# A decoder layer on one core: the opening's first attention row is served in another order

## The reference

```python
def _L0_attn_ref(x, Wv, bv, Wo, bo):
    p = jnp.einsum('bsd,ed->bse', x, Wv) + bv
    p = p.reshape(b, s, h, dk).transpose(0, 2, 1, 3)       # h = 16, dk = 8
    q = k = v = p
    attn = jax.nn.softmax(jnp.einsum('bhqd,bhkd->bhqk', q, k) / math.sqrt(dk), axis=-1)
    out = jnp.einsum('bhqk,bhkd->bhqd', attn, v)
    out = out.reshape(b, s, h * dk)                        # heads are not moved back: rows mix heads
    return jnp.einsum('bsd,ed->bse', out, Wo) + bo
x = x + _L0_attn_ref(_layernorm(x), Wv, bv, Wo, bo)
x = x + _L0_xattn_ref(_layernorm(x), ctx, ctx)             # 16 heads, no projections
x = x + _L0_ffn_ref(_layernorm(x), ...)                    # shared expert and the best of 7, SwiGLU
```

## Time and profile before

| | us |
|---|---|
| median of 3 runs (all) | 404.37 (403.18, 404.37, 407.61) |
| the profiled execution | 406.06 |
| its span, first to last instruction | 403.8 |
| TensorE busy in the span | 392.3 (97%) |
| VectorE, ScalarE, GpSimd busy | 309.7, 297.1, 283.1 |

### The profile page before, as it was taken

How to read it: one execution, slowest core, us unless ns; L and a number is a source line. 1 busy time by engine, 2 the same in 40 slices (tenths; PEclk the granted TensorE clock), 3 DMA queues, 4 the chain that set the end, 5 groups by cost and what they waited for, 6 DMA issues and landing times.

```text
span 403.8 us, 16282 instructions
## 1 busy us (share of the span) xinstructions
PE 392.3 (97%) x5549; PEld 309.9 (77%) x5550; DVE 309.7 (77%) x847; ACT 297.1 (74%) x685; POOL 283.1 (70%) x476
## 2 busy tenths in 40 slices
PE   8989999999999999899999999999999999999996
PEld 5556666666666666566666666999999999999996
DVE  7759999999999999899999987775444454455444
ACT  7568999999999999799999967622224666766651
POOL 7756888888888888688888744367777464444442
PEclk9999999999999999999999999999999999999999
DMA  6254656776777677675645400012223454520001
GB/s 105 48 81 61 100 94 99 134 117 123 126 132 123 118 122 135 124 124 98 79 54 61 36 22 5 0 48 87 87 86 101 106 144 142 143 89 21 30 32 55
DMA packets 176325, 35.22 MB, mean 87 GB/s; under 512 B 145587, under 2 KB 174646, under 8 KB 176256
## 3 DMA queue, kind: packets, MB, share of 16 engines
q1 hardware_dynamic: 71296, 21.43, 24.7%
q10 hardware_dynamic: 102144, 6.81, 16.2%
q0 software_dynamic: 2816, 6.10, 4.3%
HBM read 20.86 MB, written 15.67 MB: 90 GB/s over the span
## 4 chain that ended last, share of the span: by engine, by line
PE 80%; DMA 8%; DVE 5%; ACT 2%; issue 2%; SPq 1%; ACTq 0%; POOL 0%; DVEq 0%; POOLq 0%
PE psum L928 20%; PE psum L681 13%; PE psum L690 13%; PE psum L1033 10%; PE psum L702 8%; DMA attention_out<-on_s 3%; DMA orow<-attention_out 3%; PE psum L712 3%; PE psum L780 2%; PE psum L669 2%; PE psum L812 1%; PE psum L785 1%; PE psum L819 1%; PE psum L1085 1%; SPq L198 1%
## 5 line engine op out<-in xcount | busy, mean ns | idle before, releaser
L1743 DVE TENSOR_TENSOR gT<-gT,psum 128x384 f32<-128x384 f32 x66 | 36.6, 554 | 63.9 <-ACT gT L1375 38.1
L472 POOL TENSOR_TENSOR k_s<-pT,hmask_sb 128x1024 f32<-128x1024 f32 x32 | 60.9, 1902 | 17.2 <-issue 14.5
L642 POOL DMA_INDIRECT out<-yrow,token x38 | 37.0, 973 | 39.1 <-DVE yrow L1877 34.2
L1375 ACT ACTIVATE gT<-psum 128x384 f32<-128x384 f32 x66 | 32.1, 487 | 39.3 <-PE psum L928 38.6
L1033 PE MATMUL psum<-wdn_sb,gT 128*128 (+1 forms) x414 | 57.5, 275 | 0.0
L928 PE MATMUL psum<-fhT,wtile 128*128 128x128 f32 x456 | 57.1, 275 | 0.0
L928 PEld LDWEIGHTS psum<-fhT,wtile 128*128 128x128 f32 x456 | 53.9, 192 | 0.0
L1033 PEld LDWEIGHTS psum<-wdn_sb,gT 128*128 128x128 f32 x414 | 51.7, 192 | 0.2 <-DVE gT L1743 0.2
L928 PE MATMUL psum<-hT_all,wup_sb 128*128 128x128 f32 x384 | 48.2, 276 | 0.0
L1484 DVE TENSOR_REDUCE mx_s<-psum 128x16 f32<-128x1024 f32 x33 | 40.4, 1225 | 9.0 <-PE psum L681 6.3
L690 PEld LDWEIGHTS psum<-id_sb,pr_x 128*128 128x128 f32 x248 | 27.3, 141 | 24.5 <-ACT pr_x L1135 24.1
(11 more groups left out here) (199 smaller groups left out, 872.2 us busy)
## 6 DMA issues: line engine op xcount, KB each, us to landing
sorted_rows<-nowhere_row SPq DMA_DIRECT2D x38, 130.0 KB, 3.6
ring<-sorted_rows SPq DMA_DIRECT2D x30, 130.0 KB
wup_sb<-in_wup SPq DMA_DIRECT2D x14, 176.0 KB, 2.6
orow<-attention_out SPq DMA_DIRECT2D x31, 64.0 KB
ring<-in_ctxv ACTq DMA_DIRECT2D x60, 32.0 KB, 4.1
cross_keys<-in_ctxk ACTq DMA_DIRECT2D x14, 128.0 KB, 3.2
ring<-cross_keys SPq DMA_DIRECT2D x112, 16.0 KB
rows_all<-in_x ACTq DMA_DIRECT2D x10, 128.0 KB, 3.2
```

The source lines that it names most:

```text
L472: nc.gpsimd.tensor_tensor(k_s[:], pT[:].rearrange("p (b k) -> p b k", b=NB).unsqueeze(2).broadcast_to([P, NB, HG, S]), hmask_sb[:, 0:HG].u ...
L642: pool.indirect_dma_start(out=out, out_offset=bass.IndirectOffsetOnAxis(ap=token[p][:, 0:1], axis=0), in_=yrow[p][:, :], in_offset=None, b ...
L1743: nc.vector.tensor_tensor(g, g, ps_up[k][:, 0:CH * P], ALU.mult).then_inc(sem("f_g"), 1)
```

## The change

Four things, all in steps 3 and 4 of the opening, with line numbers moving by a few:

- SyncE stores both halves of units 0 and 1; ScalarE's `second_store` in the opening goes.
- VectorE writes `on_s` of unit 1 ahead of both subtractions of step 4, and puts `attention_added(0)` between them.
- TensorE does `project(0)` ahead of unit 2's transposes and `query(0)` right behind `new_row`; ScalarE does `output(0)` ahead of unit 2's exponentials and `query(0)` right behind `turned`.
- The fillers at the end of step 3 and those ahead of `query(0)` in step 4, two calls of two products each, go.

```diff
--- before.py
+++ after.py
@@ SyncE, body
                 if live("out") and u["out"] < U - 1:
                     sp.wait_ge(sem("s_on"), at(u["out"]))
                     store_half(sp, u["out"], 0)
+                    if t < STEADY:
+                        store_half(sp, u["out"], 1)
@@ TensorE, opening
+                if live("q"):
+                    project(u["q"])
                 if live("soft_s"):
                     turn("s", u["soft_s"], 0)
                     turn("s", u["soft_s"], 1)
-                if live("q"):
-                    project(u["q"])
                 if live("xT"):
                     new_row(u["xT"])
+                if live("q"):
+                    query(u["q"])
                 if live("soft_s"):
                     self_weighed(u["soft_s"])
...
                 if live("soft_s"):
                     turn_back("s", u["soft_s"])
-                if t == LAG["q"]:
-                    keep_clock(2, bank[3])
-                if live("q"):
-                    query(u["q"])
...
-                    keep_clock((1, 4, 4, 2)[t], bank[3])
+                    keep_clock((1, 4, 4, 0)[t], bank[3])
@@ ScalarE, opening
+                if live("q"):
+                    output(u["q"])
                 if live("soft_s"):
                     exp("s", u["soft_s"], 0)
                     exp("s", u["soft_s"], 1)
-                if live("out"):
-                    second_store(u["out"])
-                if live("q"):
-                    output(u["q"])
-                if live("soft_s"):
                     turned("s", u["soft_s"], 0)
                     turned("s", u["soft_s"], 1)
+                if live("q"):
+                    query(u["q"])
                 bulk_of_step(t)
...
                 if live("out"):
                     cross_values(u["out"], 1)
-                if live("q"):
-                    query(u["q"])
@@ VectorE, opening
                 if live("out"):
                     invert("s", u["out"])
-                if live("out") and t < LAG["q"]:
                     normalise("s", u["out"])
                 if live("soft_s"):
                     soften("s", u["soft_s"], 0)
-                    soften("s", u["soft_s"], 1)
-                if live("out") and t >= LAG["q"]:
-                    normalise("s", u["out"])
                 if live("q"):
                     attention_added(u["q"])
+                if live("soft_s"):
+                    soften("s", u["soft_s"], 1)
+                if live("q"):
                     query_moments(u["q"])
```

## The result

The changed kernel takes 408.76 us (median of 20 runs, 405.46 to 412.56) where the kernel before, beside it, takes 405.21 us (20 runs, 403.18 to 408.42): a ratio of 1.0075, 95% interval [1.0049, 1.0101]. It is slower by some 3 us, three quarters of a per cent (3.5 us between the two medians), and the time lies outside the predicted range (403.2 to 407.4). The three runs of before on which the prediction stood (404.37) lay 0.84 us under the median of twenty.

A forecast was written before the change was run, and what follows sets the result against it. The prediction took TensorE's pace in the loop to bound the kernel, with the opening's chain through unit 0's row ahead of it. +2.32 (dependency) − 0.99 (sooner row) = +1.33 us on 404.37 gave 405.7 us, range 403.2 to 407.4.

The forecast's parts named there:

- dependency: Step 4: unit 2's softmax now stands behind unit 0's projection, so unit 3's self scores end later after the row, +2.32 us.
- sooner row: Unit 0's attention output, stored by SyncE alone, is read back and turned at 25.55 instead of 26.54, -0.99 us.
- T: Start of `turn_output(0)`, when TensorE turns unit 0's row: 26.54 before, predicted 25.55, between 25.1 and 26.05.
- the fillers' 0.86 us: TensorE time of the fillers on the chain behind unit 0's row; predicted to buy nothing, as it lies beside unit 3's softmax.
- unit 1's sooner row: Unit 1, normalised ahead of step 4's subtractions, lands near 31.7 rather than 32.84; predicted to buy nothing.
- the softmax of unit 3 ends last alone: Step 5: of three chains that ended together, only unit 3's softmax still ends last; its second transposes start at 34.85, not 33.52.
- the two ahead of T fill an idle wait and cost nothing: Fillers at the end of step 3, while TensorE waits for unit 0's row: no gain counted for leaving them out.
- the rival of the clock: TensorE's clock falls in the opening without fillers and work there takes twice as long: +1.33 + 2.8, 408.5 us; chance 0.05.
- the footing: Starting time for the sum: 404.37 us, median of three timed runs of the kernel before.
- Whatever is won or lost before this loop moves the end of the kernel by the same amount: Loop over the units, 47 to 154 us, runs at TensorE's pace, so the opening's +1.33 us reaches the end.
- the absorbing rival: Later `orow` waits, 154 to 235 us, 2.5 us in all, swallow the slip: time stays 404.4 us; chance 0.10.
- the faster rival: Unit 3's scores have unseen slack, so 0.99 and 0.86 us are won: 402.5 us; chance 0.13.

The follow-up runs named there:

- a_fill34_2: Changed kernel with step 3's fillers back and two fillers between the halves of unit 2's transposes in step 4, second batch: ratio 1.0026 [0.9995, 1.0056].
- b_nofill: Kernel before without the fillers of steps 3 and 4, its order kept, first batch: ratio 1.0007 [0.9974, 1.0040].
- b_all_but_first_fill3: Kernel before with SyncE's two stores, unit 1 normalised sooner and only step 4's fillers out: ratio 0.9995 [0.9970, 1.0020].
- a_fill34_3: Changed kernel with step 3's fillers back and two between the halves of unit 2's transposes, third batch: ratio 1.0029 [0.9994, 1.0063].
- a_soft_first_fill3: Changed kernel with both of unit 2's subtractions ahead of `attention_added(0)` again and step 3's fillers back: ratio 1.0014 [0.9993, 1.0034].
- a_fill3_3: Changed kernel with only step 3's fillers back, third batch: ratio 1.0054 [1.0014, 1.0094].
- b_fill3: Kernel before without step 4's fillers, step 3's kept: ratio 0.9989 [0.9955, 1.0023].
- b_nofill_3: Kernel before without the fillers of steps 3 and 4, its order kept, in a later 405 us batch: ratio 1.0055 [1.0017, 1.0094].
- a_fill3: Changed kernel with only step 3's fillers back, first batch: ratio 1.0035 [1.0002, 1.0068].
- a_again: Changed kernel itself measured once more, against the kernel before: ratio 1.0071 [1.0028, 1.0114].
- a_again_3: Changed kernel itself measured again in a later 405 us batch, against the kernel before: ratio 1.0073 [1.0035, 1.0112].
- a_fill4: Changed kernel with two fillers in step 4 only, between the halves of unit 2's transposes: ratio 1.0049 [1.0013, 1.0086].
- b_all_but_first: Kernel before with SyncE's two stores, unit 1 normalised sooner and all four fillers out, without putting unit 0 first: ratio 1.0042 [1.0005, 1.0078].
- a_fill3_2: Changed kernel with only step 3's fillers back, second batch: ratio 1.0032 [1.0004, 1.0059].
- b_fill4: Kernel before without step 3's fillers, step 4's kept: ratio 1.0009 [0.9970, 1.0049].

## Why the prediction was wrong, and where it held

The sum was +2.32 (dependency) - 0.99 (sooner row) = +1.33 us. Taken by its steps:

**Right: the new dependency and its size.** In the profile after, measured from T = 26.25, with the predicted value behind: the row's copy ends at +0.63 (0.65), the projection at +1.17 (1.24), the second subtraction at +2.16 (2.22), the exponential at +2.83 (2.86). Beyond that the clock is down; in a_fill34_2, where it is not, the second half of the transposes ends at +3.54 (3.57) and the scores at +5.67 (5.70). `xn_s` is ready at 29.55, T + 3.30 (3.6), and holds nothing up. A chain in a new order, built from durations of the old trace, was right within 0.07 us at each step, and 0.30 us for `xn_s`.

**Right: the fillers' 0.86 us and unit 1's sooner row are worth nothing on the path**, by b_nofill and b_all_but_first_fill3, and the softmax of unit 3 ends last alone (the waits of 0.26 and 0.44 us for `pr_s` above).

**Mis-sized: the sooner row, -0.99, was -0.29.** The issue was as predicted (22.00 for 21.95). The term that failed is "the read took 4.07 us here ... I take 3.6 us": it took 4.20. The reasoning, that a read issued sooner gets ahead of the transfers behind it, did not hold in most profiles: of the twelve profiles in the new order T is 26.1 to 26.4 in eight. In the other four it is 25.18, 25.32, 25.58 and 25.80, and the read took 3.1 us or less in three of them and 3.75 in the last. So the value I chose occurs, in a minority of executions. In the three with the shortest read (a_fill34_3, a_soft_first_fill3, a_fill3_3) TensorE had no wait for the row at all; it came straight from the fillers of step 3, and how much sooner the row was there is not known.

**Wrong: "the two ahead of T fill an idle wait and cost nothing", and the rival of the clock, priced at 0.05.** This is the step that failed, beside the read. It counted only the time that the fillers take, and put at nothing what TensorE's clock does without them. In the profile after, with 1.98 us idle before T, 0.35 before the projection and 1.02 between the halves of the transposes, the clock fell to 0.50 at 28.4 us, and 34 of 44 runs of the changed kernel have a fall. The kernels with these two fillers kept the clock in the opening in every profile; that they are the cause is likely by that, and not settled (below).

I had argued against a fall from the one wait at 163.4 us, 0.02 us of work in 1.60 us at a clock of 1.00. That showed that such a wait can leave the clock alone, not that it always does: in b_fill3 it fell behind a single wait of 1.86 us, in b_nofill_3 behind one of 2.03 us, and behind one of 2.06 us in a_fill3 it did not. One row without a fall should not have brought the chance down to 0.05. The drop of the pass time from 0.44 to 0.22 us, from which I took the two levels, is real, but the trace has the granted clock of those first fillers (2 to 6 us) at 1.00, so the level there rests on the pass time alone. The Trainium skill ("TensorE: Matmul & The Clock Gate", HAM oscillation) has the rule that idle gaps on TensorE throttle it again, so that the work behind them starts at the lower clock; the waits in its example are longer than any here. The trace agrees in the direction: the scores behind the gaps took 1.96 us in place of 1.02.

Its size was too high: I wrote 2.8 us, if everything from T to T + 5.7 ran at half speed. The fall starts at T + 2.1 instead, behind the projection and half of the transposes, and `weigh` hardly slowed. The scores end at T + 7.35 where they end at T + 5.67 without it, so it costs 1.7 us where it lasts 6.8 us. In the profiles where it lasts 3.4 us (a_again, a_again_3, a_fill4) step 6 starts 16.4 to 16.8 us after T, against 15.4 to 15.5 with the clock kept: 0.9 to 1.3 us. That the rival's 408.5 lies so near the measured 408.76 is luck: its clock term was 1.1 us too large, and the row (0.70) and the footing (0.84) were off the other way.

**Not absorbed, though waits moved.** "Whatever is won or lost before this loop moves the end of the kernel by the same amount" held within 0.7 us: 3.68 us more at step 6, 4.38 us more at the end. On the way the waits behind 154 us did shrink (2.5 to 1.5 us), as the absorbing rival had it, but 1.9 us of waits came up ahead of 154 us, where the loop had none. And the faster rival needed T at 24.2; the soonest seen is 25.18, with fillers ahead of it.

**The account.** Predicted 405.7, measured 408.76, 3.06 us apart. Of these 0.84 is the footing (three runs for twenty), 0.70 the row (26.25 for 25.55), and 1.7 the clock as in the profiled execution: 3.2 together. That this comes out so closely is partly luck, since row and clock are those of one execution (410.44 us), 1.7 us above the median, and one run in four kept its clock. From the side of the runs: the ten of the changed kernel's 44 that kept the clock have a median of 406.0 us, against 404.7 and 405.2 for before's runs of that kind in two batches, so about 1 us for the dependency and the row together, close to the +1.33 of the sum; the rest comes from the runs with a fall. By kernels: fillers out of the old order 1.0055 [1.0017, 1.0094]; new order with both groups back 1.0026 to 1.0032 in three batches, none of whose intervals excludes 1 by itself. Each is a part of 1.0075, and their sum agrees with it within the intervals; these are wide, and the first ratio was 1.0007 [0.9974, 1.0040] in b_nofill's batch.

**What stays open.** (1) Step 3's fillers kept the opening's clock in each of 11 profiles, yet 8 of 12 runs of a_fill3_3 had a fall somewhere. Only one execution of a set is profiled, so whether those falls were in the opening, or near 105 to 117 us as in two other profiles, isn't known. The share of each group of fillers is therefore not settled, only that with both out falls are more frequent (8 of 12 for b_nofill_3, against 5 of 29 runs of before beside it). Nor is it known why the runs of b_nofill_3 and b_all_but_first that kept their clock are slow too. (2) A run with a fall is longer than the opening's fall explains. Of the changed kernel's 44 runs the ten that kept the clock have a median of 406.0 us; eleven with a mean clock of 0.994 to 0.996, as the profiles with a fall of 3.4 us have it, 408.2; twenty at 0.990 to 0.992, as in the profile with 6.8 us, 410.1. The opening accounts for 0.9 to 1.7 us of this. For the kernel before (408.4 to 408.5 us with a fall, 404.7 to 405.2 without) the 3.4 us of a long wait and a fall in the loop, as in b_fill3, would be of the right size; none of its runs with a fall was profiled in a 405 us batch.

## What to carry to other kernels

A filler in a wait that is there anyway costs next to nothing and may be holding the clock. Before it is taken out, price a fall behind the wait from durations of the same products at either level, and judge the kernel without it by the mean clock of many runs: one profile of b_nofill kept its clock, and in another batch 8 of 12 runs of the same kernel did not. When an instruction is moved ahead of another chain, the chain that it is put in front of inherits its wait; here unit 2's softmax had been using the very wait for unit 0's row. Time taken from one of three chains that end together is worth only what the other two also give.

## What the runs showed of the hardware that was not expected

- The same kernel with the same gaps keeps its clock in some executions and loses it in others: 34 of 44 runs of the changed kernel have a fall, and over its three profiles it starts at 28.2 to 29.3 us and lasts 3.4 or 6.8 us. The Trainium skill ("TensorE: Matmul & The Clock Gate", The HAM clock gate) says of the rise behind a kernel's start that its moment varies from run to run, since the chip's look at the activity is not aligned with the kernel; the three profiles show such a spread for a fall in the middle of one.
- A single wait between two full stretches can be enough: the clock fell behind 1.86 us (b_fill3, 117 us) and 1.85 us (a_fill3_2, 105 us), and stayed at 1.00 behind 1.88 us (b_fill4) and 2.06 us (a_fill3).
- At the lower clock not every product takes twice as long: self scores 1.99 us for 1.09, `weigh`, 32 small products, 1.08 for 0.96.
- Two stores of one tile, one behind the other from SyncE, land 2.60 us after the second issue; from SyncE and ScalarE it was 2.55 us. Giving up the second queue cost nothing to be seen.
- The read of unit 0's row takes from 3.1 us or less to 4.3 us over the profiles for the same 64 KB, and of a sooner issue (22.00 for 22.43) most is lost again to a longer read; what sets its length wasn't found.
- Whole batches stand at 405 or at 419 us for all kernels alike, on one chip in both conditions, with a fall of the clock at 276 to 283 us in the second; what sets this wasn't found.
